# Out-of-range indices for empty edge slots in the gathers of a two-layer graph attention kernel

## The reference

```python
# graph convolution, then layer norm
x = layernorm(x + segment_sum(h[row] * norm[:, None], col) + b)      # h = x @ W, self loops added
# relational graph attention, twice (4 heads, ELU between, then 1 head), then layer norm
def rgat_conv(x, W, q, k, b, src, dst, etype, heads, out_ch, n_nodes):
    xr = jnp.einsum('nd,rdf->rnf', x, W)          # one table of rows per relation
    oi, oj = xr[etype, dst], xr[etype, src]
    alpha = leaky_relu(oi @ q + oj @ k, 0.2)
    e = exp(alpha - segment_max(alpha, dst)[dst])
    a = e / (segment_sum(e, dst)[dst] + 1e-16)
    msg = (a[:, :, None] * oj.reshape(-1, heads, out_ch)).reshape(-1, heads * out_ch)
    return segment_sum(msg, dst) + b
x = layernorm(x + rgat_conv(elu(rgat_conv(x, W1, ...)), W2, ...))
```

## Time and profile before

| | |
|---|---|
| median of 3 runs | 1627.22 us (1626.15 to 1629.14) |
| profiled execution | 1631.22 us, its span 1629.4 us |
| TensorE busy | 1398.5 us, 86% of the span |
| VectorE busy | 1135.4 us, 70% |
| ScalarE busy | 401.9 us, 25% |
| POOL busy | 390.5 us, 24% |
| DMA, POOL's queue | 28,160 packets, 139.52 MB, 25.5% of 16 engines' span |
| DMA, SP's queue | 77,551 packets, 160.68 MB, 31.1% |

### The profile page before, as it was taken

One profiled execution on the slowest core, in us unless ns is written; L12 is line 12 of the kernel. 1 busy time (PEld: TensorE's weight loads), 2 busy tenths in 40 slices (PEclk: granted clock), 3 DMA queues, 4 the chain that ended last, 5 costly groups with the idle time before them and its releaser, 6 DMA issues. The chain is left out here.

```text
span 1629.4 us, 23071 instructions
## 1 busy us (share of the span) xinstructions
PE 1398.5 (86%) x7239; PEld 1101.7 (68%) x7239; DVE 1135.4 (70%) x2394; ACT 401.9 (25%) x1013; POOL 390.5 (24%) x389
## 2 busy tenths in 40 slices
PE   3699978878878688999599999939998995999991
PEld 2467734545545378999599999936998993555550
DVE  4988788788787359998388888771555333666667
ACT  2023202233333212111244444352222210000002
POOL 1000000000000100000477777400000006777750
PEclk8889998989989898999799999958998997999996
DMA  9054221122223197663799999605664558999973
GB/s 257 21 175 165 107 79 43 62 70 88 91 70 104 59 335 223 184 197 103 251 314 328 319 321 309 185 0 178 183 185 134 189 166 292 324 323 322 321 229 94
DMA packets 105814, 301.51 MB, mean 185 GB/s; under 512 B 17677, under 2 KB 47183, under 8 KB 105663
## 3 DMA queue, kind: packets, MB, share of 16 engines
q1 hardware_dynamic: 77551, 160.68, 31.1%
q0 software_dynamic: 28160, 139.52, 25.5%
HBM read 245.31 MB, written 57.18 MB: 186 GB/s over the span
## 5 line engine op out<-in xcount | busy, mean ns | idle before, releaser
L1276 DVE CUSTOM_DVE_ANT_0 fl_early<-fl_masks,fl_gap 125x1250 bf16<-125x1250 f32 x120 | 166.9, 1451 | 23.9 <-DMA fl_masks<-fl_d_k 19.3
L815 PE MATMUL fr_ps<-fr_col_hot,fr_row_hot 125*128 x516 | 121.5, 367 | 49.7 <-DVE fr_col_hot L553 44.3
L1169 POOL DMA_INDIRECT xH<-fl_d_xr,edge_row x88 | 95.8, 1089 | 252.6 <-DMA fl_d_xr<-fl_xs 221.5
L1169 POOL DMA_INDIRECT xH<-sl_d_xr,edge_row x88 | 87.0, 989 | 271.1 <-DMA sl_d_xr<-sl_xs 241.8
L860 PE MATMUL fr_ps<-fr_h,fr_shared 125*125 125x384 f32 x400 | 142.5, 505 | 1.7 <-DVE fr_shared L581 1.7
L1547 PE MATMUL sl_ps<-xH,sl_hot 128*125 128x386 f32 x352 | 118.5, 494 | 17.6 <-DVE sl_hot L1350 17.6
L1543 PE MATMUL fl_ps<-xH,fl_masks 128*125 128x194 f32 x704 | 121.1, 331 | 11.4 <-DVE fl_masks L1343 10.5
L1507 PE MATMUL fl_ps<-fl_wH,xH 128*125 128x384 f32 x360 | 122.4, 340 | 9.7 <-ACT fl_xs L1190 9.7
L1226 ACT ACTIVATE fl_masks<-fl_plain,fl_ex 128x125 f32<-128x125 f32 x352 | 106.8, 385 | 93.9 <-PE fl_ps L1543 74.8
L1507 PE MATMUL sl_ps<-sl_wH,xH 128*125 128x384 f32 x360 | 124.6, 346 | 5.9 <-DVE sl_wL L1266 5.9
L1543 PEld LDWEIGHTS fl_ps<-xH,fl_masks 128*125 128x125 f32 x704 | 117.1, 189 | 12.6 <-issue 12.6
(11 more groups left out here) (269 smaller groups left out, 2532.9 us busy)
## 6 DMA issues: line engine op xcount, KB each, us to landing
fr_raw<-in_w SPq DMA_DIRECT2D x36, 384.0 KB, 3.7
fl_wH<-d_dl SPq DMA_DIRECT2D x22, 512.0 KB, 6.3
sl_before<-d_dl SPq DMA_DIRECT2D x22, 512.0 KB, 4.3
fl_d_xr<-fl_xs SPq DMA_DIRECT2D x60, 169.8 KB
sl_d_xr<-sl_xs SPq DMA_DIRECT2D x60, 168.9 KB
d_gap<-fr_gap SPq DMA_DIRECT2D x30, 312.5 KB, 2.5
fl_gap<-d_gap SPq DMA_DIRECT2D x30, 312.5 KB, 3.6
sl_before<-d_gap SPq DMA_DIRECT2D x30, 312.5 KB, 3.5
```

The lines of the kernel that those rows point to most:

```text
L815: mm = pe.matmul(ps[:, par + h, 0:HC], row_hot[:, bass.ds(slot, 1), s, :].rearrange("p o n -> p (o n)"), col_hot[:, bass.ds(slot * TG + s, ...
L1169: pool.indirect_dma_start(rows(c // 4)[:, c % 4], None, d_xr, bass.IndirectOffsetOnAxis(ap=edge_row[:, c:c + 1], axis=0)).then_inc(gathere ...
L1276: v.tensor_tensor_reduce(dump[:, i % 2], krow[0:P, h * R + q % R], gap_all[0:P, q % GR], 1.0, -3e38, ALU.subtract, ALU.max, mk[:, q // R, ...
```

## The change

Two places change. Where the list is unpacked, 3750 (R x N, the number of rows in the table) is added to `edge_row` in empty slots, whose row index was 0. The indirect transfers get a bound of 3749: a row with a greater index isn't transferred, and that is no error. Its place in the ring keeps what was there. The weight of such a slot is 0 as before.

```diff
@@ -609,7 +609,8 @@
             def unpack_rows():
                 v.wait_ge(dst_made, 1)
                 link(v.scalar_tensor_tensor(out=s_row, in0=s_rel, scalar=float(N), in1=s_src, op0=ALU.mult, op1=ALU.add))
-                v.tensor_copy(edge_row[:], s_row).then_inc(unpacked, 1)
+                link(v.tensor_scalar(s_key, slot_dst[:], 0.0, float(R * N), ALU.is_equal, ALU.mult))
+                v.tensor_tensor(edge_row[:], s_row, s_key, ALU.add).then_inc(unpacked, 1)
                 v.tensor_scalar(empty[:], slot_dst[:], 0.0, NO_EDGE, ALU.is_equal, ALU.mult).then_inc(unpacked, 1)
 
             def unpack_relation(r):
@@ -1167,7 +1168,8 @@
                 if c >= 4 * QR and c % 2 == 0:
                     pool.wait_ge(pair_done, (c - 4 * QR) // 2 + 1)
                 pool.indirect_dma_start(rows(c // 4)[:, c % 4], None, d_xr,
-                                        bass.IndirectOffsetOnAxis(ap=edge_row[:, c:c + 1], axis=0)).then_inc(gathered[c // 4 % QR], 16)
+                                        bass.IndirectOffsetOnAxis(ap=edge_row[:, c:c + 1], axis=0),
+                                        bounds_check=R * N - 1, oob_is_err=False).then_inc(gathered[c // 4 % QR], 16)
```

## The result

The changed kernel takes 1635.04 us (median of 6 runs) against 1627.37 us for the one before on the same chip: ratio 1.0042, 95% interval 1.0029 to 1.0055. It is slower by 0.42%. Its profiled execution took 1632.5 us (span 1630.7).

The account below looks back on a forecast made before the run. TensorE was taken to bound the attention layers, the DMA engines close behind but hidden. Terms of -2.2 (end stalls), 0 (bound) and 0 (list) took 1627.22 to 1625.0 us; range over all 1622.5 to 1646, the forecast's own 1623.0 to 1627.3.

Parts of the forecast that it names:

- rival A: Attention layers: the bound test slows POOL's gather issue and POOL takes TensorE's place; +18 us at 0.1 us per issue; chance 0.34.
- Part 1: Ends of both attention layers: skipped row fetches let the last gathers land sooner, removing TensorE stalls of 1.05 and 1.16 us, -2.21 us.
- Part 2: POOL's gather issue in both attention layers: the bound adds no time to an issue, 0 us.
- x: Change of POOL's time for one gather issue due to the bound; taken as 0, with 0.32 us as upper end.
- its formula: Rival A's price: 16 opening issues, plus 168 more per layer beyond spare 5.4 (second) and 9.4 us (first), less 2.2.
- Part 3: Front, where the list is unpacked: 0.37 us of added VectorE work hides behind 0.84 us of idling, costing 0.
- B: Gathers: skipped rows still travel as something just as long, or land no sooner; no gain, 1627.2 us; with D 0.09.
- C: First attention layer's middle: three small TensorE stalls go too as the queue carries 11% less; -3.4 us, 1623.5; chance 0.10.
- D: Gathers: the index isn't over the bound or the bound isn't applied; B's time, 1627.2 us; with B 0.09.

Follow-up runs that it names:

- e14: The whole change with its bound held in a register instead of a MOVE ahead of each gather, against the kernel before: 1628.19 us, ratio 1.0017.
- e13: The kernel before plus the bound on every gather, held in a register set once per layer, nothing skipped: 1631.73 us, ratio 1.0033.
- e2: The kernel before, no bound, with empty slots fetching row 29 times their partition instead of row 0: 1624.63 us, ratio 0.9975.
- e9: Same kernel as e13 (bound in a register, nothing skipped), in an earlier group, against the kernel before: 1631.62 us, ratio 1.0031.
- e11: The kernel before with VectorE making the previous quad's selector ahead of its wait for gathers, and different rows for empty slots, no bound: 1613.35 us, ratio 0.9920.
- e10: The kernel before, no bound, with POOL writing a small column ahead of each gather and waiting for that write: 1647.57 us, ratio 1.0128.
- e12: The kernel before plus the constant bound on every gather, a MOVE ahead of each, nothing skipped: 1640.95 us, ratio 1.0087.
- e8: The change as it is, timed again in another group with shifted semaphore counts, against the kernel before: 1631.97 us, ratio 1.0031.
- e3: The kernel before with bound and out-of-range index in the last 12 of 176 chunks alone: 1625.71 us, ratio 0.9983.
- e15: The kernel before with VectorE's loop turned, and bound and out-of-range index in the last 12 chunks alone: 1615.53 us, ratio 0.9929.
- e4: Same kernel as e13 (bound in a register, nothing skipped), on a chip with slower gathers, against the kernel before: 1660.53 us, ratio 1.0004.

## Why the prediction was wrong

It forecast 1625.0 us by its likeliest case and came out slower than before, inside the range and by rival A.

**Part 1, the transfers: right.** The stall before the last two quads is gone in both layers, the rates of 219 and 237 GB/s have no place any more, and the bytes fell by 15.6 MB where "some 15" stood. The size fits within the intervals: 2.21 us forecast, 3.5 us of medians (e14 against e13) or, by the ratios, 0.16% of 1627, 2.6 us. That the price lay in the one row more than in the bytes, which the prediction left open, is shown by e2.

**Part 2, the bound: this is the step that failed.** It said: "I take x = 0, the value of the median row, because the instruction takes the same 0.95 us whether it fetches 128 different rows or row 0 128 times". The runs show x = 0.051 us, and medians of 998 to 1002 ns in every kernel with a bound on every gather. The argument was about the wrong variable: that the time doesn't depend on which rows are fetched says nothing about a step that is added for each index. The Trainium skill's rule ("DMA: Bandwidth & Descriptors", SWDGE vs HWDGE vs iDMA: a core runs code that computes a descriptor pair per operation) pointed to x above 0, and the measured 51 ns for 128 indices agrees.

**Rival A named the mechanism, but its price was too low, for two reasons.** At x = 0.051 its formula gives 16 x 0.051 = 0.8 for the openings, 168 x 0.051 - 5.4 = 3.2 in the second layer, nothing in the first, less 2.2: +1.8 us. Measured is +7.7.

- The room of a whole layer can't be counted. The formula let POOL's spare time in a whole layer (9.4 us in the first) pay for lateness anywhere in it. But VectorE's wait for quad q holds up the selector of quad q - 1, so TensorE stalls when one quad is late by more than POOL is ahead at that moment, and POOL can be ahead by the ring of four quads at most. Room farther off is no help. (This is argued from the waits in e9 and e13, where POOL still waits for TensorE 4 to 5 us a layer, the usual 0.30 us of each gap included, while TensorE loses 3 to 6 us; in e11, with the loop turned and no bound, the small stalls are nearly gone.) In the first layer the formula has no loss at 0.051; e13 has 259.29 us there against 254.57, and e9 256.89. With the 0.077 of e10 the formula gives 16 x 0.077 = 1.2, and 12.9 - 5.4 = 7.5 and 12.9 - 9.4 = 3.5: 12.3 us, and 20.7 were measured. At 0.051 without the skipping the formula gives +4.0 where e13 and e9 measured +5.8 and +4.8, so near its start it isn't far off. (The price at which rival A passes 0.2% is also slightly off: at x = 0.056 its sum is 0.9 + 4.0 - 2.2 = 2.7 us, 0.17%.)
- The MOVE. The prediction knew only the instruction's own time. The MOVE of a constant bound, 29 ns and not visible in the median interval, lets POOL start 0.76 us instead of 0.26 behind each wait for TensorE, comes with longer gathers here and there, and costs 0.54% without the skipping (e12 against e13). With the skipping it is less: 0.31 to 0.42% for the change (e8 and its first timing) against 0.17% for e14, in other groups and with intervals that meet.

Together: e14 has +2.3 us where the formula gives +1.8 for the change without a MOVE; the rest of the change's +7.7 (or of the +5.1 of e8) is put down to the MOVE. No group has the change and e14 side by side.

**Part 3, the list: right.** The added steps in the front, on VectorE's timeline:

```profile
231.40 0.25 DVE L612 TENSOR_SCALAR fr_shared<-slot_dst 128x176 f32<-128x176 f32 x1
231.68 0.34 DVE L613 TENSOR_TENSOR edge_row<-fr_shared 128x176 int32<-128x176 f32 x1
...
232.93 0.42 DVE L549 TENSOR_TENSOR fr_row_hot<-fr_io_col,fr_row_key 125x256 f16 x1 [0.74 <-issue]
```

VectorE still idles 0.74 us before its next selector, against 0.84.

**The other rivals.** B falls: skipped gathers land 2.1 us after their issue at the least, against 4.3. C, that the first layer's small stalls (1.2 us) would go because the queue carries less, isn't seen: the change has 6.03 us idle there, e14 1.91 and e3 1.55. The least, 0.99, is in e2, which carries as many bytes as before. D falls with the bytes.

**What stays open.** Why some gathers, mostly 16 apart, are longer, and what sets how long (up to 1.76 us with the MOVE, up to 1.65 in e10, e11 and e15 without bound or MOVE there, at most 1.25 in the second layer of e9, e13 and e14): the runs measure it and don't name the cause. Also the change's own form with the loop turned wasn't run, so how much of the MOVE's price the turned loop would hide isn't known.

## What to carry to other kernels

When an instruction gets an option that must be decided per element, don't read its price from how little the time depends on the data; take it as above zero and ask first how much spare time its engine has in each round of the loop, not over the stage: spare time elsewhere pays for nothing while a later round's wait stands ahead of work that is ready. If padding has to be fetched, ask for many different rows before spending anything on not fetching it, and put an option only where it earns something. A constant passed to an instruction in a loop may cost an instruction of its own each time; hold it in a register. Look also at which instruction carries the wait: here it moved from the transfer to the MOVE ahead of it.

## What the hardware showed that I had not expected

- A bound on an indirect transfer of 128 rows costs GpSimd 51 ns per issue, (947 to 998 ns), whether any row is out of range or not. If it is spent per index, which no run varied, that is an estimated 0.4 ns each.
- A register MOVE of 29 ns ahead of each such transfer leaves the median interval at 1303 ns and still costs 9.2 us over 352 gathers (e12 against e13). A wait ahead of the transfer is then ahead of the MOVE, and the transfer starts 0.76 us or more after what it waited for, instead of 0.26.
- Some transfers, mostly 16 apart, take longer. In the kernel before it is every 16th of the second layer, the 24th, the 40th and so on, with 1.27 us. With a bound and a MOVE it is up to 1.76 us and mostly one chunk earlier (the 23rd, the 39th). Without either it is up to 1.65 us in e10, e11 and e15. With the bound in a register three or four are over 1.12 us, and none over 1.25 (e9, e13, e14).
- Gathers whose 128 indices name the same row of HBM run at 219 to 237 GB/s at 94 to 95% busy engines. With 128 different rows in the empty slots the same stretch of the second layer runs at 288 (e2), and full chunks in the middle of a layer at 318 to 326.
- The same kernel moves 286 GB/s in the middle of the second layer in group 2 (e4) and 325 in group 3 (e9), each on its own chip, and the kernel before takes 1660 against 1627 us. Which engine ends last, and so whether this change costs anything, differs with it: the bound in a register costs 0.04% there and 0.31 to 0.33% in groups 3 and 4.
- A small GpSimd write between two indirect transfers doesn't lengthen the interval (1252 ns with it, 1254 without), and lengthens it by 77 ns once it is waited for.
